# A fused attention block on one core: turn 2 keeps TensorE's transposes, B is loaded in two column halves, denominators are scaled at another place, the tiles' score products alternate

## What is computed

```python
x = x + softmax(LN(x) @ ctx.T) @ ctx                  # cross attention, 25088 keys
x = x + attn(LN(x))      # 32 query heads, 8 key/value heads, width 64; softmax over d x e of each token
x = x + ffn(LN(x))       # LN(x) @ W_base.T + b_base, plus 8 experts of rank 16, the top 2 of a router
# attn:  scores = einsum('bsdh,bseh->bsde', q, k) / 8;  out = einsum('bsde,bseh->bsdh', softmax(scores), v)
# ffn:   h = einsum('bnd,erd->bner', x, A);  delta = einsum('bner,eor->bno', h * route, B)
```

## Time and profile before

| | |
|---|---|
| median of 3 runs | 2446.21 us (2444.52 to 2447.72) |
| the profiled execution | 2443.54 us, its span 2442.0 us |
| busy: TensorE, VectorE | 2399.8 us (98%), 2042.5 us (84%) |
| busy: ScalarE, GpSimd | 1101.5 us (45%), 1389.7 us (57%) |
| DMA | 544.46 MB, mean 223 GB/s |
| a turn, in the middle of the kernel | 43.5 us, TensorE busy throughout |

### The profile page before, as it was taken

One profiled execution on the slowest core, in us unless ns is written; L12 is line 12 of the kernel. 1 busy time (PEld: TensorE's weight loads), 2 busy tenths in 40 slices (PEclk: granted clock), 3 DMA queues, 4 the chain that ended last, 5 costly groups with the idle time before them and its releaser, 6 DMA issues.

```text
span 2442.0 us, 35933 instructions
## 1 busy us (share of the span) xinstructions
PE 2399.8 (98%) x11070; PEld 1971.0 (81%) x11070; DVE 2042.5 (84%) x2800; ACT 1101.5 (45%) x1577; POOL 1389.7 (57%) x1052
## 2 busy tenths in 40 slices
PE   6999999999999999999999999999999999999999
PEld 5788888888888888888888888888888888877777
DVE  8888889888888898888988889898888988974466
ACT  4444444444444444444444444444444444433553
POOL 2666666666666565664655556566465555651541
PEclk9999999999999999999999999999999999999999
DMA  9988989989899989989999998998999999789643
GB/s 231 264 219 221 249 229 229 246 220 244 232 229 245 235 224 242 228 225 238 235 229 236 234 220 227 242 230 222 239 234 229 236 236 223 214 181 194 176 130 100
DMA packets 488311, 544.46 MB, mean 223 GB/s; under 512 B 72902, under 2 KB 362694, under 8 KB 485832
## 3 DMA queue, kind: packets, MB, share of 16 engines
q1 hardware_dynamic: 478280, 501.90, 84.5%
q0 software_dynamic: 9984, 41.95, 5.2%
HBM read 488.71 MB, written 30.41 MB: 213 GB/s over the span
## 4 chain that ended last, share of the span: by engine, by line
PE 87%; DVE 4%; DMA 2%; issue 2%; POOL 2%; SPq 1%; ACT 1%; DVEq 0%; POOLq 0%; ACTq 0%
PE ps L1518 29%; PE ps L1519 28%; PE ps L1520 28%; POOL nat_lo L632 2%; DMA raw<-in_ctx_dram 1%; SPq L534 1%; DMA quads<-probs 1%; DVE ch_lo L1101 1%; DMA tr<-wt_dram 1%; SPq L495 1%; DVE tr L1097 1%; ACT nat_hi L792 0%; PE ps L1546 0%; DVE acc L1238 0%; DMA x_in<-in_x_dram 0%
## 5 line engine op out<-in xcount | busy, mean ns | idle before, releaser
L632 POOL TENSOR_TENSOR nat_lo<-raw,nat_hi 128x512 fp32r<-128x512 f32 x784 | 1146.5, 1492 | 859.0 <-ACT nat_hi L792 822.1
L1101 DVE TENSOR_TENSOR ch_lo<-tr,ch_hi 128x512 fp32r<-128x512 f32 x784 | 748.1, 954 | 220.2 <-ACT ch_hi L781 219.0
L781 ACT CAST ch_hi<-tr 128x512 fp32r<-128x512 f32 x784 | 478.0, 622 | 723.0 <-PE ps L1520 574.7
L1518 PE MATMUL ps<-ch_hi,xt_hi 128*128 128x512 f32 x1696 | 665.7, 392 | 15.5 <-DVE ch_lo L1101 13.2
L1519 PE MATMUL ps<-ch_lo,xt_hi 128*128 128x512 f32 x1696 | 661.4, 390 | 0.0
L1520 PE MATMUL ps<-ch_hi,xt_lo 128*128 128x512 f32 x1696 | 661.1, 390 | 0.0
L1518 PE MATMUL ps<-nat_hi,pt_hi 128*128 128x512 f32 x1568 | 611.1, 390 | 3.2 <-DVE pt_lo L1042 1.8
L1519 PE MATMUL ps<-nat_lo,pt_hi 128*128 128x512 f32 x1568 | 610.7, 389 | 0.0
L1520 PE MATMUL ps<-nat_hi,pt_lo 128*128 128x512 f32 x1568 | 610.5, 389 | 0.0
L1097 DVE STREAM_TRANSPOSE tr<-quart 128x512 f32<-128x512 f32 x784 | 548.3, 700 | 0.9 <-DMA quart<-in_ctx_dram 0.9
L792 ACT CAST nat_hi<-raw 128x2048 fp32r<-128x2048 f32 x196 | 374.9, 1913 | 191.4 <-PE ps L1520 174.9
(11 more groups left out here) (205 smaller groups left out, 1364.0 us busy)
## 6 DMA issues: line engine op xcount, KB each, us to landing
quart<-in_ctx_dram SPq DMA_DIRECT2D x392, 512.0 KB, 8.4
raw<-in_ctx_dram SPq DMA_DIRECT2D x196, 1024.0 KB, 9.1
quads<-probs SPq DMA_DIRECT2D x376, 64.0 KB, 2.9
wq_in<-in_L_attn_Wq_dram POOLq DMA_DIRECT2D x16, 1024.0 KB, 6.4
win<-in_L_ffn_W_base_dram SPq DMA_DIRECT2D x64, 256.0 KB, 12.5
tr<-wt_dram POOLq DMA_DIRECT2D x64, 256.0 KB, 3.6
wt_dram<-stage SPq DMA_DIRECT2D x32, 256.0 KB, 5.7
wt_dram<-stage_b SPq DMA_DIRECT2D x32, 256.0 KB, 10.2
```

The lines of the kernel that those rows point to most:

```text
L632: last = pool.tensor_tensor(nat_lo[:, j, t], raw[:, j % 2, t], nat_hi[:, j, t].bitcast(F32), ALU.subtract)
L781: act.copy(ch_hi[:, c % RING_CH, :], tr[:, c % RING_TR, :]).then_inc(chunk_hi, 1)
L1101: dve.tensor_tensor(ch_lo[:, c % RING_CH, :], tr[:, c % RING_TR, :], ch_hi[:, c % RING_CH, :].bitcast(F32), ALU.subtract).then_inc(chunk_s ...
L1518: pe.matmul(out_, a_hi, b_hi, start=start, stop=False)
```

## The change

1. `by_dma` is false for turn 2 too. Its probabilities are transposed by PE behind chunk 1 and late piece 7; SP moves none in the turn before, and the count that VectorE waits for begins one turn later.
2. B is loaded in two column halves, each with eight DMAs of half the size. The half that does not lie over `quads` goes behind turn 47's moves, the other stays where all of B was.
3. `rescale` stands directly behind the split of the probabilities (after chunk 5, in turn 1 after chunk 7), ahead of that step's chunk transpose, and no longer waits for the accumulator.
4. `pair_scores` goes through the matrices m in the outer loop and the tiles in the inner one.

```diff
-                self.by_dma = not (self.first or self.second or self.over)
+                self.by_dma = not (isinstance(i, int) and 2 * i + 1 + step <= 2 or self.over)
...
-                for q in range(TT):
-                    move_next_probs(turn, q)
+                if not (turn.first or turn.second):
+                    for q in range(TT):
+                        move_next_probs(turn, q)
...
-            def load_expert(e):
-                sp.dma_start(b_nat[:, :, e * RANK:(e + 1) * RANK],
-                             lora_b[e].rearrange("(o p) r -> p o r", p=P)).then_inc(b_loaded, 16)
+            def load_experts(half):
+                cols = slice(half * CH, (half + 1) * CH)
+                for e in range(EXPERTS):
+                    sp.dma_start(b_nat[:, cols, e * RANK:(e + 1) * RANK],
+                                 lora_b[e].rearrange("(o p) r -> p o r", p=P)[:, cols]).then_inc(b_loaded, 16)
 
             next_block(REST[0], LAST_M)
+            load_experts(1)
...
             sp.wait_ge(lo_drained, G_PT + TT * (NB - 1))
-            for e in range(EXPERTS):
-                load_expert(e)
+            load_experts(0)
...
             def rescale(turn):
 
-                dve.wait_ge(acc_updated, turn.times(8, 2 - 8))
                 dve.wait_ge(denom_ready, turn.times(1))
...
-                dve.wait_ge(probs_moved[q], turn.times(16 * QR, -16 * QR))
+                dve.wait_ge(probs_moved[q], turn.times(16 * QR, -2 * 16 * QR))
...
                         for q in range(TT):
                             probs_group(turn, q)
+                        rescale(turn)
                     n = c + AHEAD
                     if n < DC or not turn.last:
                         transpose_chunk(turn.times(DC, n), n, turn.times(16 * QR, 16 * QR * (n // DC)))
-                    if c == 7 and not turn.first:
-                        rescale(turn)
...
-                    if c == 3 and turn.second:
+                    if c == (3 if turn.second else 1) and not (turn.first or turn.by_dma):
                         for q in range(TT):
                             probs_group(turn, q)
...
-                for t in range(TT):
-                    for m in range(8 * o, 8 * o + 8):
+                for m in range(8 * o, 8 * o + 8):
+                    for t in range(TT):
...
-                        pe.wait_ge(b_loaded, 16 * EXPERTS)
+                        pe.wait_ge(b_loaded, 2 * 16 * EXPERTS)
```

## The result

The changed kernel takes 2431.7 us (median of 4, 2430.9 to 2432.2) beside 2446.0 for the kernel before: a ratio of 0.9945, 95% interval 0.9933 to 0.9958. The prediction was 2433.7, in a range from 2428 to 2440. The profiled execution took 2430.85 us, against a forecast of 2431.0 for it.

A forecast was written before the change was run, and what follows sets the result against it. TensorE, busy in 98% of the span, was taken as the bound. Terms -7.4 - 0.5 - 2.3 - 2.3 = -12.5 us took the profiled 2443.5 to 2431.0; with 2.7 to the median, 2433.7 us, range 2428 to 2440.

The forecast's parts named there:

- Turn 2: Window 100:150: the whole 8.3 us hole goes, eight PE transposes cost 0.9, net -7.4 us.
- the hole closes in part: Turn 2: chunk 6 or 8 comes 3 us late, the clock falls again, 3.5 us remain: 2437.6; chance 0.13.
- the slower rival: Denominators' new place: POOL's burst there makes the pair cost 2.4 us, chunk 6 stalls in 46 turns, about 2521; chance 0.06.
- Denominators: Pair moved ahead of chunk 8's transpose: stalls ahead of chunk 8 go, chunk 6 loses some; net -0.5 us, from -2.5 to +4.
- 0.27 fits nearly everywhere, and the nine lose about 0.22 each: +2.0: Chunk 6: the pair's 0.27 us fits its distance except in nine turns where moved probabilities land late; +2.0 us.
- B in halves: End: half of B loaded a turn earlier, row piece 2 lands sooner, PE's 3.2 us go; -2.3 us, bounds 0 and -4.5.
- that chain moves by 2.3 and no more: End: DVE's unbroken work from late piece 7 to Wk's split, which PE awaits, comes only 2.3 us sooner.
- Score products: Alternating tiles make a group of 16 take 0.45 us instead of 0.59; 16 groups, -2.3 us, bounds 0 and -3.2.
- the prediction's estimate: Score products, if the bank rule held: 16 starts of 0.032 and the last one's length, 0.70 a group, +1.8 in all.
- The sum: Whole kernel: turn 2, denominators, B and score products, -7.4 - 0.5 - 2.3 - 2.3 = -12.5 us.

The follow-up runs named there:

- 7.1 by the part alone: Kernel before with only turn 2's probabilities transposed by TensorE: ratio 0.9971 (0.9960 to 0.9983), 7.1 us.
- the kernel with the loads moved alone: Changed kernel with, in odd late turns, the next base-matrix row loads issued behind the probabilities' moves; denominators' place unchanged: ratio 0.9920, 2427.5 us.
- +1.9 in the part alone: Kernel before with only the denominators' pair moved and its accumulator wait dropped: ratio 1.0008 (0.9997 to 1.0019), median 2450.4 against 2448.4.
- the doubled pair: Changed kernel with two more unused 128x2 operations behind the denominators' first one in every turn: ratio 1.0029, 20.5 us slower than the changed kernel.
- the second trace of the kernel after: Changed kernel itself, unchanged, timed again beside the kernel before and profiled a second time: ratio 0.9952 (0.9936 to 0.9969), 2434.7 us.
- 4.9 by the part alone: Kernel before with only B loaded in two halves: ratio 0.9980 (0.9969 to 0.9990), 4.9 us.
- 2.9 alone: Kernel before with only the order of the score products changed: ratio 0.9988 (0.9979 to 0.9997), 2.9 us.

## Where the prediction was right and wrong

**Turn 2** (-7.4; measured -7.56, and 7.1 by the part alone). Right in each step: PE transposes in 1.03 us, ACT and DVE done in time, no wait for moved probabilities before turn 3, 222 matmuls in the window. The rival "the hole closes in part" isn't dead, though. Of nine traces in which TensorE turned turn 2's probabilities and nothing was added to DVE, six have 0.9 us and three have 2.0, 2.4 and 3.0, with 0.8 to 1.8 us of PE idle ahead of chunk 6. Its 0.13 was too little for a single execution, and its price of 3.5 us too high for these. In two of the three the pair stands where the change put it, and a row piece that landed 1.2 to 1.5 us later pushed DVE so far that the pair fell into POOL's burst. DVE and POOL in turn 2 of the kernel with the loads moved alone:

```profile
102.09 0.72 DVE L1132 TENSOR_TENSOR denom_s<-denom,alpha 128x2 f32<-128x2 f32 x1
102.85 1.23 DVE L1134 TENSOR_TENSOR denom<-denom_s,row_sum 128x2 f32<-128x2 f32 x1
...
101.50 2.55 POOL L635 TENSOR_TENSOR nat_lo<-raw,nat_hi 128x512 fp32r<-128x512 f32 x2 [2.62 <-DMA wq_dram<-wq_out]
```

The pair takes 1.98 us there, 2.45 in the other trace, and 0.33 in the two of the kernel after. That is the mechanism of the slower rival, in one turn.

**Denominators** (-0.5; measured +1.35 in the two traces, +1.9 in the part alone, and within the scatter both times). The pair's price was nearly right, 0.33 us against 0.27. The stalls ahead of chunk 8 went: 2.5 us in the trace that I read, 2.1 to 6.9 in the five of the table. What was mis-sized is the other side, "0.27 fits nearly everywhere, and the nine lose about 0.22 each: +2.0". With the pair moved the turns stand 7.1 to 10.1 us ahead of chunks 6 and 7, with it at its old place 2.9 to 7.1: by the means 4.0 more, double the 2.0. The step took the distances at chunk 6 in one trace for fixed. Odd late turns have theirs set by when the moves land, which falls otherwise in each execution, from 0.05 to 0.7; whatever is put ahead of chunk 6 then costs in those turns in full. And early turns that looked free lost up to 0.10 each in the kernel after. Gain and loss came out equal, so the -0.5 for the sum isn't refuted, and isn't shown. The slower rival's mechanism (POOL at the new place) didn't occur in turns 3 to 47 of any trace, where the pair takes 0.35 us from start to end; but the doubled pair shows that the edge was at least as near as that rival put it: 0.39 us more cost 20 us.

**B in halves** (-2.3, bound -4.5; measured -5.34 in the end, -3.75 in the second trace of the kernel after, +2.12 in the middle, 4.9 by the part alone). Row pieces 2 and 3 landed earlier and PE's two waits went, as said. The step that failed is "that chain moves by 2.3 and no more". Counted from the start of turn 48, late piece 7 is added 51.67 us later before and 49.71 after, 2.0 sooner and near the forecast; but the last split of Wk, for which PE waits before, ends at 88.95 and 85.17, 3.8 sooner. The 1.8 in between come from how DVE's operations meet POOL's. Timelines of both, before:

```profile
2175.79 5.27 POOL L681 TENSOR_TENSOR nat_lo<-w_rows,nat_hi 128x512 fp32r<-128x512 f32 x4 [7.92 <-ACT nat_hi L869]
2183.00 7.53 POOL L681 TENSOR_TENSOR nat_lo<-w_rows,nat_hi 128x512 fp32r<-128x512 f32 x4 [1.94 <-ACT nat_hi L869]
...
2179.93 1.68 DVE L1238 SCALAR_TENSOR_TENSOR acc<-acc,old_scale,x_nat 128x512 f32<-128x512 f32 x1
...
2183.04 3.38 DVE L1262 TENSOR_TENSOR nat_lo<-w_rows,nat_hi 128x2048 fp32r<-128x2048 f32 x1
```

and POOL after, to be held against the last two DVE rows of the end above:

```profile
2165.74 5.58 POOL L684 TENSOR_TENSOR nat_lo<-w_rows,nat_hi 128x512 fp32r<-128x512 f32 x4 [9.00 <-ACT nat_hi L872]
2173.64 7.95 POOL L684 TENSOR_TENSOR nat_lo<-w_rows,nat_hi 128x512 fp32r<-128x512 f32 x4 [2.32 <-ACT nat_hi L872]
```

The first of these two DVE operations now begins at 2171.35, when POOL's first burst is over, and takes 0.74 instead of 1.68; the second begins 0.12 ahead of POOL's second burst instead of 0.04 behind it, and takes 2.27 instead of 3.38. With the denominators' pair 0.63 shorter and two x_nat operations 0.95 longer that makes 1.7 of the 1.8. What this split of 128x2048 takes hangs on 0.1 us in all fourteen traces: in eight it starts 0.12 ahead of POOL's burst and takes 2.27; in four it starts 0.03 to 0.05 behind and takes 3.38; and in two it starts 0.03 behind and takes 2.27, while POOL's first operation takes 3.4 instead of 1.3. I moved a chain of DVE as if its durations went with it. The other 1.5 us of the end are the slow piece of the clock, which I hadn't looked for behind the earlier trace rows.

**Score products** (-2.3; measured -2.71, 2.9 alone). Right: 16 x 0.15 = 2.4 of it is the groups themselves (the forecast's own 16 x 0.14 is 2.2, rounded up to 2.3). The rule of the Trainium skill, TensorEngine Tiling (Array Packing), "Gotcha 1: PSUM Pressure", that different row tiles can't access one PSUM bank at the same time, would by the prediction's estimate have made it 0.70 us a group. The trace says 0.44: here the measurement decides against it.

**The sum.** -12.5 predicted, -12.7 measured in the profiled executions. Denominators and the middle cost 4.0 us more than I said, B 3.0 less in the end; the start, the products and turn 2 gave the rest. In the second trace of the kernel after the same sum is -8.2, since turns 3 to 47 and the end fell worse. By time the change is worth 11.7 and 13.5 us, from the ratios 0.9952 and 0.9945. So the hit to a few tenths is luck; the sign, turn 2 and the products are not.

## What to carry to other kernels

An operation's own price says little: taking 101 us from DVE bought nothing that could be measured, since what was won ahead of chunk 8 was lost ahead of chunk 6. Look up the distance between the maker and the taker of each chunk, and its smallest value over several turns, before something is put in front of it.

Where a small move of data is on the path and large loads aren't, issue it first: four loads of 256 KB placed behind eight moves of 64 KB brought 6 to 8 us here (ratio 0.9920 against the 0.9945 and 0.9952 of the kernel after). The kernel before has the same order of loads; what it would win alone there was not tried.

One trace is one throw. The distances that transfers set scatter from execution to execution, and only edits tried alone and timed in several rounds said which part a microsecond belonged to.

## What the runs showed that I had not expected

What a DVE operation with two inputs from SBUF takes hangs on POOL: 0.65 and 1.72 us for the same split of a chunk, 0.74 and 1.68 for a multiply-add of 128x512, 2.27 and 3.38 for 128x2048, and 0.16 and 1.2 for 128x2. A small operation pays as much as a large one, and 0.1 us in the order of the two starts can be worth 1.

TensorE's slow pieces in the end and the middle last 3.4 us each and don't always follow a hole. Before, PE's last wait ahead of the one in the end is over at 2195.33; in windows of 2 us the clock falls at about 2214. PE has no idle time ahead of that, but it makes four bias products, which multiply 4 rows instead of 128 (PE's timeline, then the windows):

```profile
2212.35 1.98 PE L1645 MATMUL ps<-side_rows,ones 4*128 4x512 f32 x4
```

```profile
2212.00:2214.00 2.00, 2.00 (x6) 0.66 (x4) 2.00 (x2) 1.74 (x3) 0.00 (x0) 1.00 1.08 226
2214.00:2216.00 2.00, 2.00 (x6) 1.38 (x6) 2.00 (x4) 2.00 (x4) 0.00 (x0) 0.64 1.07 222
```

In seven of the nine traces with a slow piece in the end, one begins 0.8 to 2 us behind the last of these four products. The five traces without one make the same products, so they don't bring it by themselves.

Two row tiles of 48x64 that write one bank run beside each other: sixteen in 0.44 us when they alternate, 0.59 when eight follow eight.
